# Moving the eviction of half the queries to VectorE and reordering work around it, in a gated two-layer attention and expert kernel

## The reference

```python
x = x + tanh(g_xattn[0]) * L0_xattn(layernorm(x), ctx, ctx, W, b)       # one head, 256 wide
x = x + tanh(g_ffn[0])   * L0_ffn(layernorm(x), Wg, Wu, Wd)             # 8 experts, each silu(x@Wg)*(x@Wu)@Wd, summed
x = x + tanh(g_xattn[1]) * L1_xattn(layernorm(x), ctx, mask, gamma, beta, Wq, Wkv, Wout)
x = x + tanh(g_ffn[1])   * L1_ffn(layernorm(x), wg, W, b)               # top-1 of 8 experts, 256 tokens each at most
```

```python
q = xn @ Wq * 64 ** -0.5                  # [2048, 512]
k, v = split(ctx @ Wkv)                   # 154 keys
attn = softmax(where(mask, q @ k.T, -inf) - rowmax)
out  = (attn @ v) @ Wout
```

## Time and profile before

| | before |
|---|---|
| median of 3 runs | 1287.86 us (1285.17 to 1289.67) |
| the profiled execution's own time | 1287.86 us |
| its span in the trace | 1286.1 us, granted clock 0.989 |
| busy: PE / DVE / ACT / POOL | 97% / 71% / 50% / 43% of the span |
| second attention and routed experts | from about 1048 us on |

### The profile page before, as it was taken

How to read it: one execution, slowest core, us unless ns; L and a number is a source line. 1 busy time by engine, 2 the same in 40 slices (tenths; PEclk the granted TensorE clock), 3 DMA queues, 4 the chain that set the end, 5 groups by cost and what they waited for, 6 DMA issues and landing times.

```text
span 1286.1 us, 17755 instructions
## 1 busy us (share of the span) xinstructions
PE 1244.6 (97%) x6212; PEld 1010.3 (79%) x6212; DVE 909.8 (71%) x1655; ACT 642.1 (50%) x1360; POOL 550.9 (43%) x542
## 2 busy tenths in 40 slices
PE   7999999999999999999999999999999999999994
PEld 5778888888888888888888888888888887778773
DVE  5987777777777677777777777777777674767654
ACT  2455555554555455454555455454555445545542
POOL 3635654444444444444444444444444024443424
PEclk9999999999999999999999999999999999999988
DMA  4100300000000000110000000000000130000031
GB/s 135 50 1 1 116 25 26 25 25 25 25 25 25 25 25 26 41 34 25 25 25 25 25 25 25 25 26 25 25 25 1 49 115 1 18 34 2 34 102 60
DMA packets 41672, 44.21 MB, mean 34 GB/s; under 512 B 4140, under 2 KB 40048, under 8 KB 41455
## 3 DMA queue, kind: packets, MB, share of 16 engines
q1 hardware_dynamic: 37984, 38.87, 9.2%
q0 software_dynamic: 1488, 3.57, 0.8%
q10 hardware_dynamic: 2111, 0.63, 0.2%
HBM read 35.27 MB, written 8.32 MB: 34 GB/s over the span
## 4 chain that ended last, share of the span: by engine, by line
PE 88%; DVE 5%; ACT 3%; issue 1%; POOL 1%; DMA 0%; another core or an unknown queue 0%; ACTq 0%; DVEq 0%; POOLq 0%
PE bank L1072 25%; PE bank L1071 25%; PE bank L1073 25%; ACT PC L832 2%; PE bank L1276 2%; PE bank L1285 2%; PE bank L1432 1%; DVE nmC L1733 1%; PE bank L1260 1%; PE bank L1368 1%; PE bank L1210 1%; PE bank L1215 1%; PE bank L1211 1%; PE bank L1237 1%; PE bank L977 0%
## 5 line engine op out<-in xcount | busy, mean ns | idle before, releaser
L1071 PE MATMUL bank<-xop_hi,w_hi 128*128 128x512 f32 x896 | 351.4, 392 | 1.7 <-ACT half_g L763 1.2
L1072 PE MATMUL bank<-xop_lo,w_hi 128*128 128x512 f32 x896 | 352.2, 393 | 0.0
L1073 PE MATMUL bank<-xop_hi,w_lo 128*128 128x512 f32 x896 | 351.3, 392 | 0.0
L1677 DVE TENSOR_TENSOR acc<-bank,acc 128x512 f32<-128x512 f32 x248 | 170.8, 689 | 119.8 <-PE bank L1073 119.4
L1663 DVE TENSOR_TENSOR hid_lo<-hid,hid_hi 128x512 fp32r<-128x512 f32 x256 | 213.6, 855 | 34.7 <-ACT hid_hi L786 34.6
L1071 PE MATMUL bank<-hid_hi,wd_hi 128*128 128x512 f32 x512 | 202.4, 395 | 0.6 <-DVE hid_lo L1663 0.6
L1072 PE MATMUL bank<-hid_lo,wd_hi 128*128 128x512 f32 x512 | 203.0, 396 | 0.0
L1071 PEld LDWEIGHTS bank<-xop_hi,w_hi 128*128 128x128 f32 x896 | 168.6, 188 | 42.8 <-ACT half_g L763 1.5
L1073 PE MATMUL bank<-hid_hi,wd_lo 128*128 128x512 f32 x512 | 201.4, 393 | 0.0
L1072 PEld LDWEIGHTS bank<-xop_lo,w_hi 128*128 128x128 f32 x896 | 168.5, 188 | 38.4
L1073 PEld LDWEIGHTS bank<-xop_hi,w_lo 128*128 128x128 f32 x896 | 168.4, 188 | 37.4
(11 more groups left out here) (216 smaller groups left out, 1770.7 us busy)
## 6 DMA issues: line engine op xcount, KB each, us to landing
raw_gu<-in_L_ffn_Wg_dram SPq DMA_DIRECT2D x32, 256.0 KB, 2.7
raw_gu<-in_L_ffn_Wu_dram SPq DMA_DIRECT2D x32, 256.0 KB, 3.2
raw_d<-in_L_ffn_Wd_dram SPq DMA_DIRECT2D x32, 256.0 KB, 3.6
slots<-empty_row SPq DMA_DIRECT2D x1, 2080.0 KB, 10.7
xr<-slots SPq DMA_DIRECT2D x8, 260.0 KB, 4.4
x_res<-in_x_dram SPq DMA_DIRECT2D x4, 512.0 KB, 5.2
we_raw<-in_L_ffn_W_dram SPq DMA_DIRECT2D x8, 256.0 KB, 4.1
out_dram<-x_res SPq DMA_DIRECT2D x3, 512.0 KB
```

What stands on the lines that cost most here:

```text
L1071: mm(ps, w, a, start=start, stop=False, skip_group_check=True)
L1072: mm(ps, w, a_low, start=False, stop=False, skip_group_check=True)
L1073: return mm(ps, w_low, a, start=False, stop=True, skip_group_check=True)
L1677: nc.vector.tensor_tensor(out=to, in0=ps, in1=to, op=ALU.add).then_inc(acc_added, 1)
```

## The change

It has five parts.

1. ACT evicts only banks 0 and 2 of the queries, DVE evicts 1 and 3 (`q_out(f, 1)` between `route_variances` and `route_normed`, `q_out(f, 3)` behind `route_normed`). The semaphore `c_q` is split in two, and PE waits for both.
2. POOL's set-up: the first `power` goes ahead of the wait and the subtraction for `Wq_lo`; all of `keep_own_heads(0)` goes behind the second `power`.
3. POOL issues two scatters, not one, ahead of the routing `power`.
4. `o_out` of tile 2 goes from ACT to DVE, behind `front_normed`. ACT's `pT_out(c, 2, 0)` goes behind `exps(c, 3, 0)`.
5. In chunks with routing, PE's `p_transposes(c, 1, (1, 2))` goes behind the wait for `r_shift` and `project(c, 0)`, and DVE's `add_attention(c, 0)` goes ahead of `pT_out(c, 1, 1)`, as both are in chunk 0 already.

```diff
@@ POOL, chunk and set-up
-                    scatter(c - 1, range(1) if front else range(CT))
+                    scatter(c - 1, range(2) if front else range(CT))
...
-                    scatter(c - 1, range(1, CT))
+                    scatter(c - 1, range(2, CT))
...
             nc.gpsimd.tensor_copy(Wq_hi[:], Wqs[:]).then_inc(consts_ready, 1)
+            power(LN_FRONT, CT, 1)
             pool.wait_ge(consts_ready, 5)
             nc.gpsimd.tensor_tensor(out=Wq_lo[:], in0=Wqs[:], in1=Wq_hi[:].bitcast(F32), op=ALU.subtract).then_inc(consts_ready, 1)
-            power(LN_FRONT, CT, 1)
-            keep_own_heads(0, range(2))
             power(LN_FRONT2, CT, 1)
-            pool.wait_ge(c_ln, 1)
+            keep_own_heads(0)
             x_low(0)
-            keep_own_heads(0, range(2, 3))
-            keep_own_heads(1, range(3))
+            keep_own_heads(1)
@@ ACT
-                for m in range(HB):
+                for m in range(0, HB, 2):
                     act.wait_ge(c_q_ps, HB * f + m + 1)
-                    nc.scalar.mul(qT[:, m, :], bank[SIM[m]][:], HD ** -0.5).then_inc(c_q, 1)
+                    nc.scalar.mul(qT[:, m, :], bank[SIM[m]][:], HD ** -0.5).then_inc(c_q_act, 1)
...
-                    if j == CT - 2:
-                        pT_out(c, j, 0)
                     exps(c, j + 1, 0)
-                    if j < CT - 2:
-                        pT_out(c, j, 0)
+                    pT_out(c, j, 0)
                     exps(c, j + 1, 1)
                     pT_out(c, j, 2)
-                    if j == CT - 2:
-                        o_out(c, j)
@@ PE
-                    wait_apart(c_q, HB * c + 2 * half + 2)
+                    wait_apart(c_q_act, 2 * c + half + 1)
+                    pe.wait_ge(c_q_dve, 2 * c + half + 1)
...
                 if route:
-                    p_transposes(c, 1, (1, 2))
                     pe.wait_ge(r_shift, r + 1)
                 project(c, 0)
-                if not route:
-                    p_transposes(c, 1, (1, 2))
+                p_transposes(c, 1, (1, 2))
@@ DVE
+            def q_out(f, m):
+                dve.wait_ge(c_q_ps, HB * f + m + 1)
+                nc.vector.tensor_scalar(qT[:, m, :], bank[SIM[m]][:], HD ** -0.5, None, ALU.mult).then_inc(c_q_dve, 1)
...
-                if with_route:
-                    pT_out(c, 1, 1)
-                    add_attention(c, 0)
-                else:
-                    add_attention(c, 0)
-                    pT_out(c, 1, 1)
+                add_attention(c, 0)
+                pT_out(c, 1, 1)
...
                     front_normed(f)
+                o_out(c, 2)
...
                 route_variances(c)
+                q_out(f, 1)
                 route_normed(c)
+                q_out(f, 3)
...
             front_normed2(0)
+            q_out(0, 1)
+            q_out(0, 3)
```

More of the change, by code:

```diff
@@ L330, in flamingo_kernel @@
         c_prep_ps, c_prep_act = sem("c_prep_ps"), sem("c_prep_act")
-        c_yT_ps, c_ln, c_xnT_ps, c_xnT, c_xn_lo, c_q_ps, c_q, c_x2 = (
-            sem(n) for n in ("c_yT_ps", "c_ln", "c_xnT_ps", "c_xnT", "c_xn_lo", "c_q_ps", "c_q", "c_x2"))
+        c_yT_ps, c_ln, c_xnT_ps, c_xnT, c_xn_lo, c_q_ps, c_q_act, c_q_dve, c_x2 = (
+            sem(n) for n in ("c_yT_ps", "c_ln", "c_xnT_ps", "c_xnT", "c_xn_lo", "c_q_ps", "c_q_act", "c_q_dve", "c_x2"))
         c_sim_ps, c_nmax, c_probs, c_rden, c_norm, c_pT_ps, c_pT_act, c_pT_dve, c_o_ps, c_o, c_out_ps, c_res = (
@@ L550, in v_masks, with keep_own_heads @@
                 ins.then_inc(consts_ready, 1)
-            def keep_own_heads(b, groups):
-                for g in groups:
-                    of = P_BLOCKS[g]
+            def keep_own_heads(b):
+                for g, of in enumerate(P_BLOCKS):
                     pool.wait_ge(c_prep_act, C_VALUES + 3 * b + g + 1)
@@ L857, in route_exp @@
                 nc.scalar.activation(rt["e"][:, ts, :], rt["d"][:, ts, :], ACT.Exp).then_inc(r_exp, 1)
-            def o_out(c, j):
-                act.wait_ge(c_o_ps, c * CT + j + 1)
-                nc.scalar.copy(oT[:].rearrange("p k t -> p (k t)"), bank[5][:]).then_inc(c_o, 1)
             def chunk(c, front, route):
```

## The result

The changed kernel takes 1294.72 us (median of 6 runs, 1294.28 to 1300.03), the kernel before 1287.32 us (6 runs, 1284.71 to 1289.67). The two medians differ by 7.4 us. The ratio of the times is 1.0067, which is 8.6 us, with a 95% interval of 1.0050 to 1.0085, or 6.4 to 10.9 us: slower. The forecast was 1299.0, slower by 11.1. The profiled execution after took 1291.54 us (span 1289.8, granted clock 0.990) and is the lowest of its kernel, so the two traces differ by 3.7 us only. I therefore compare stretches of them, not spans.

The account below looks back on a forecast made before the run. No engine bounds the stage: latency along the PE, ACT, DVE and POOL loop does. Set-up 3.2, transitions 3.0, chunks 2.9 and clock 2 make 11.1 on 1287.86, so 1299.0 us (+0.86%); 8-in-10 range 1292.5 to 1304.

Parts of the forecast that it names:

- first transition: First transition inside the loop: `q_out(1)` and `q_out(3)` in the vector engine's queue delay `maxes`, +0.7 us.
- second, third transition: Second and third transitions: two scatters delay the routing power and norm, then `maxes`; +1.15 us, the third slightly less.
- TensorE's order: Inside chunks: six transposes between `project(0)` and `attend(1)`; net +0.26 us in chunks 1 and 2, +0.66 in chunk 3.
- o_out(2) with ACT's order: Inside chunks: copy behind norms that ACT's order delays holds up `project(2)`; +0.65 us in chunks 1 and 2.
- clock: Set-up: an idle of 3.2 us brings TensorE's clock to half speed for 3.4 to 6.8 us; +2 us.
- part 4: Inside the chunks: TensorE's order, ACT's order and the moved `o_out(2)`; +2.9 us, bounds +1.5 to +4.
- Part 1: Set-up, GpSimd's order: norms stretch beside `Wq_lo` and the three multiplications, TensorE starts later; +3.2 us.
- Rival A: Set-up hidden: vector engine wins the ports or norms pass between GpSimd's operations, no clock term; 1293.8 us, chance 0.17.
- Parts 2 and 3: Transitions: split of the queries' eviction and two scatters ahead of the routing power delay `maxes`; together +3.0 us.
- Rival B: Transitions: TensorE's waits for the fourth bank also bring the clock down, three times 1.7 us; 1304, chance 0.10.
- Rival C: No change that shows: set-up hidden and the exponentials' loop absorbs most of the transitions; 1290.8 us, chance 0.09.
- Rival D: Faster: exponentials start 1.0 us earlier in each of four chunks, -4.1 us, other parts hidden; 1283.8, chance 0.04.

Follow-up runs that it names:

- q2: Kernel before with the split of the queries' eviction and two scatters ahead of the routing power; 1288.25 us (9 runs), ratio 1.0036.
- c3: Kernel before with `exps(3, 0)` ahead of `pT_out(2, 0)` in every chunk; 1283.91 us (one run) beside 1285.94.
- b2: Kernel before with `dens(c, 2, 1)` behind `route_choice`, and `exps(3, 0)` ahead of `pT_out(2, 0)` in chunk 0 alone; 1284.93 us (11 runs), ratio 0.9995.
- s2: Changed kernel with GpSimd's set-up order put back as before; 1288.75 us (6 runs), ratio 1.0046.
- s3: Changed kernel with `keep_own_heads(0)` held back until the second norm is done; 1291.47 us (6 runs), ratio 1.0060.
- q3: Kernel before with two scatters ahead of the routing power, nothing else; 1287.61 us (one run) against 1283.58.
- c1: Kernel before with TensorE's and the vector engine's order of part 5 of the change alone; 1286.62 us (one run) beside 1285.94.
- c2: Kernel before with the copy of tile 2, `o_out(2)`, alone moved from ACT to the vector engine; 1287.97 us (one run) beside 1285.94.
- s1: Kernel before with GpSimd's changed set-up order alone; 1288.72 us (9 runs) against 1283.91, ratio 1.0039.
- q4: Changed kernel with both of the vector engine's query copies and the first maxima ahead of `route_normed`; 1297.88 us (6 runs), ratio 1.0109.
- b1: Kernel before with the reciprocal `dens(c, 2, 1)` behind `route_choice`; 1282.26 us (12 runs) against 1283.58, ratio 0.9986.
- s4: Changed kernel with 14 unread products on TensorE ahead of the set-up's transposes, to fill its idle; 1294.79 us (6 runs), ratio 1.0096.

## Why the prediction was right in sign and too high in size

Term by term, in us; "runs" is the ruler or the distance named.

```
                                     forecast   runs
set-up: norms beside GpSimd           +3.2      +3.18  (a)
set-up transition                     +0.1      0 (attend(0) at 10.52 in q2, as in c3, b2)
chunk 0                               +0.2      about +0.15 (c: s2, s3 less q2)
first transition                      +0.7      +0.68
second, third transition              +1.15 +1.0   +1.17 +0.93
TensorE's order, chunks 1, 2, 3       +0.26 +0.26 +0.66   +0.26 +0.26 +0.65
o_out(2) with ACT's order, 1, 2, 3    +0.65 +0.65 +0.2    +0.45 +0.44 +0.15
clock                                 +2        +1.1 in b, about -0.5 in c
```

The transitions are read at the start of `attend(0)` behind the low-part products: 10.52, 10.51, 10.50 before, 11.20, 11.68, 11.43 after. TensorE's order is the further growth up to `attend(1)`, and the last line of part 4 the growth from there to `project(2)`.

- **Part 1 held to the hundredths**: first the stretched norm beside `Wq_lo`, then L1480 back at its usual 0.17, then one norm caught by each of three multiplications. The norms' end was forecast for 1064.0 and TensorE's start for 1064.05; they came at 1063.69 and 1063.83, of which 0.16 is the earlier start of the first norm. The Trainium skill (SBUF — State Buffer, "Who interferes with whom") says that issue order decides; by the trace, `Wq_lo` and the first norm started 0.05 us apart, and GpSimd's operation lost nothing (2.35 us, 2.39 before). Rival A is out.
- **Parts 2 and 3 held.** The maxima were late by 0.60, 1.08 and 0.95. VectorE's query copies took 0.685 us, as the copies of the earlier trace rows do (0.688), without the 0.05 more that the prediction allowed for. One sentence was wrong: that the scatter's delay of the norm had been free. Alone it already moves the scores of tile 1 by 0.37 and 0.31 (q3); it made no difference to the sum, which took both together.
- **Part 4** held for TensorE's order in the sum, with some luck in chunks 1 and 2: 0.66 less 0.40 was forecast, 0.76 less 0.51 came (c1), and the two errors cancel. **The term of `o_out(2)` with the ACT order was mis-sized**: +1.5 over chunks 1 to 3 against 1.04. ACT's copy behind the exponentials costs almost nothing by itself (c3: 0.05, where "up to 0.5" stood), and the moved copy 0.2 (c2); together they give 0.45. The rest, 0.2, is the coupling, and there the mechanism was wrong. The prediction had ACT's order delay the norms by 0.2 to 0.5. They start 0.7 earlier, meet `normalise`, stretch to 2.28 and end 0.2 later, with the copy behind them. No run has these two edits alone together; the reading rests on c2, c3 and the rows after.
- The order was to cost 9.1 (3.2 + 3.0 + 2.9). The measured terms come to 3.18 + 0.15 + 2.78 + 1.17 + 1.04 = 8.3.
- One sum of the prediction doesn't come out: its own upper ends give 1287.86 + 3.2 + 3.0 + 4 + 3.3 = 1301.4, where 1302.5 stands. Nothing else hangs on it.
- **The clock, +2, was mis-sized.** The fall in the set-up came, in all three profiles with an idle of 3.16 us there (after, s1, q4) and in none of the eleven others. It cost 1.1, 2.3 and 1.1, against 1.7 to 3.3 forecast. The length was as forecast (3.4 us after, 6.8 in s1); but the forecast charged half of it, as if every product took twice as long, and in the trace after the query products start 0.43 us apart at the lower level and 0.23 at the full one. In c the changed kernel has about 0.5 less of falls than before (40.17 against 40.51, with 0.15 of order in it), so the profiled pair differs by 0.6 for it.
- Order and clock make up the 8.93 of the ruler. The measured difference, 7.4 by the medians and 8.6 by the ratio (6.4 to 10.9), agrees with that. The two profiled spans differ by only 3.7, because what follows `project(2)` of chunk 3, where nothing was edited, is 5.1 shorter after: 0.7 up to the last `project`, 2.2 from its end to TensorE's last product (39.1 before, 36.9 after; the fourteen profiles range from 36.5 to 39.1), and 2.2 from there to the end. The clock is a part of it at most: it was low for 6.8 us there before and for 3.4 after, but c1, c2 and c3 have 3.4 too and take 38.2. The rest stays open. At the very end the kernel before waits 4.74 us ahead of its last addition, for something that its trace doesn't name.
- Rival B, falls in the transitions, is neither right nor out: none in the profile after, but in s3 and q2 behind an idle of 1.35 us in the second one, in q2 again behind one of 1.18 in the third, and in q4 with one of 2.26 in the third. The longer wait isn't needed for it: in s1 and b1 the clock also fell in the third transition (s1 0.68, b1 0.83 over the ten microseconds from 1200), where TensorE's idles of 0.7 and 0.46 us are those of the kernel before, which had 1.00. In the second transition it costs 1.5 (ACT's copy to the scores of tile 1: 8.03 against 6.53), near the 1.7 given. Rival C is out by every row of d and e. Rival D's mechanism exists in chunk 0 alone, as written, and is worth 0.6 there, not 1.0.

What stays open: whether falls inside the transitions are more frequent with the longer waits; and why the copy behind `attend(3)` of chunk 3 starts 2.76 to 2.98 us after it in five profiles (before, c1, c2, c3, b2) and 2.28 in the others, with the same instructions around it and, in the kernel before, a clock of 1.00 in that window.

How far the clock blurs a comparison shows in the times. Twenty executions of the unchanged kernel on one chip, ordered by the mean granted clock of each:

```
clock 0.994          1279.37 to 1279.87   6 runs
clock 0.991          1282.33 to 1282.90   4 runs
clock 0.988 to 0.990 1284.26 to 1284.90   5 runs
clock 0.986          1287.24 to 1287.73   5 runs
```

At like clocks the orders' prices come out of the times too. s2 at 0.991 takes 1287.6 to 1289.1 (five runs) against 1282.3 to 1282.9, so about +6, where the ruler says 0.15 + 1.41 + 1.87 + 1.73 = 5.2. q2 at 0.989 takes 1287.2 to 1289.0 (six runs) against 1284.3 to 1284.9, so about +3.5, where the transitions say 2.8.

## What to carry to other kernels

When work goes from a waiting engine to a "free" one, write down the receiver's queue at that moment, with everything that its neighbours can put ahead of it; here that gave each transition to a tenth of a microsecond, while the 7 us of copies that left ACT (8 of 0.60 and 4 of 0.59) bought nothing. A wait that is removed at one consumer goes to the next one in order of issue (q4), so ask who the second consumer is before moving it. And if executions scatter by 8 us with the clock, judge edits of 1 us by distances between fixed instructions in stretches at full clock, which repeat to 0.05 us, and the sum by the times.

## What the runs showed of the hardware that I had not expected

- Some vector-engine operations that meet a GpSimd one come out just behind it, whatever their own length: norms of 0.35 us (in a row) about 0.15 us behind, and copies and products of 0.16 to 0.19 us 0.02 to 0.04 us behind, so that they take 0.93 (L1815 in c2) or 1.02 us (L1787 before). Copies from PSUM don't: the query copy at 1156.02 after takes its 0.69 us beside GpSimd's power of 1.06 at 1155.97. GpSimd's operations hardly change (`Wq_lo` 2.35 and 2.39, three multiplications 2.72 together, where 1.07, 1.07 and 0.61 make 2.75).
- In the twenty executions above the mean granted clock takes few values (0.986, 0.988 to 0.991, 0.994), and with it the time of one unchanged kernel takes four narrow levels 2 to 3 us apart. On another chip fifteen executions spread more evenly from 1280.2 us (0.996) to 1288.9 (0.986).
- TensorE's clock fell at every idle of 3.16 us at the set-up and, in two of five profiles that have it (q2 and s3, not after, s2 and s4), behind an idle of 1.35 us in the second transition. The eight transposes right behind the 3.16 us took 1.06 us in one trace (after, where the clock was 1.00 until 1065 and low from there on) and 1.94 in another (s1, where it was low from 1060.3 on, before the idle ended at 1061.11), so the same gap was paid at different places.
